# RWKV attention and mixture of experts on one core: three of four value mixes moved ahead of the weighing

## The reference

```python
shifted = pad(hidden, ((0,0),(1,0),(0,0)))[:, :-1]
key   = hidden * mix_k + shifted * (1 - mix_k)
value = hidden * mix_v + shifted * (1 - mix_v)
rec   = hidden * mix_r + shifted * (1 - mix_r)
k, v, r = key @ Wk, value @ Wv, sigmoid(rec @ Wr)
rwkv = wkv(time_decay, time_first, k, v)   # a scan over time: num and den, decayed, with a running maximum
x = layernorm(x + (r * rwkv) @ Wo)
# then, for 8 experts of width 16, the two best by a softmax router
x = layernorm(x + sum_e gate_e * (silu(x @ down_e) @ up_e))
```

## Time and profile before

| | us |
|---|---|
| median of 3 runs | 463.04 (462.94 to 463.28) |
| the profiled execution | 463.04 |
| its span | 461.3 |
| TensorE busy | 446.1 |
| VectorE busy | 405.6 |
| ScalarE busy | 355.6 |
| GpSimd busy | 315.0 |

### The profile page before, as it was taken

One profiled execution on the slowest core, in us unless ns is written; L12 is line 12 of the kernel. 1 busy time (PEld: TensorE's weight loads), 2 busy tenths in 40 slices (PEclk: granted clock), 3 DMA queues, 4 the chain that ended last, 5 costly groups with the idle time before them and its releaser, 6 DMA issues.

```text
span 461.3 us, 6679 instructions
## 1 busy us (share of the span) xinstructions
PE 446.1 (97%) x1984; PEld 339.9 (74%) x1984; DVE 405.6 (88%) x615; ACT 355.6 (77%) x801; POOL 315.0 (68%) x301
## 2 busy tenths in 40 slices
PE   8999999998999999999999999999999999999993
PEld 3444656776888878888888888888888888888761
DVE  5989998879988999999899999989898996975976
ACT  1666766785788888888788897888798887768695
POOL 2454776397758798579967797569965695754334
PEclk9999999999999999999999999999999999999997
DMA  8603220033000032100420032100420022400016
GB/s 236 222 0 118 91 91 1 1 95 112 1 1 0 2 136 92 47 0 32 153 92 0 1 137 92 48 0 23 148 93 14 1 69 93 136 1 0 0 48 227
DMA packets 20244, 30.64 MB, mean 66 GB/s; under 512 B 2032, under 2 KB 7152, under 8 KB 20208
## 3 DMA queue, kind: packets, MB, share of 16 engines
q1 hardware_dynamic: 20208, 30.21, 19.7%
HBM read 21.82 MB, written 8.39 MB: 65 GB/s over the span
## 4 chain that ended last, share of the span: by engine, by line
PE 56%; POOL 7%; DVE 7%; ACT 4%; issue 3%; POOLq 0%; ACTq 0%; DVEq 0%
PE PH L442 4%; PE PV L325 4%; PE PV L329 4%; PE PV L326 4%; PE PR L329 4%; PE PP L352 4%; PE PP L353 4%; PE PP L357 4%; PE PK L325 4%; PE PR L325 4%; PE PK L329 4%; PE PK L326 4%; PE PR L326 4%; PE PT L424 2%; ACT EX L583 2%
## 5 line engine op out<-in xcount | busy, mean ns | idle before, releaser
L583 ACT ACTIVATE PR<-PR 128x512 f32<-128x512 f32 x128 | 74.4, 582 | 24.5 <-PE PR L311 7.9
L1195 POOL TENSOR_TENSOR DQ<-DEN,EX 128x512 f32<-128x512 f32 x32 | 41.3, 1290 | 21.1 <-DVE DEN L862 21.1
L1201 POOL TENSOR_SCALAR NM<-SUM,RS 128x1 f32<-128x1 f32 x30 | 8.6, 285 | 60.1 <-ACT RS L583 60.1
L916 DVE SCALAR_TENSOR_TENSOR KT<-D,VEC,XT 128x512 f32<-128x512 f32 x57 | 47.2, 874 | 0.0
L325 PE MATMUL PK<-KH,WKH 128*128 128x512 f32 x112 | 46.2, 413 | 0.6 <-DVE NUM L879 0.6
L325 PE MATMUL PR<-RH,WRH 128*128 128x512 f32 x112 | 44.6, 399 | 1.6 <-DVE RW L903 1.6
L325 PE MATMUL PV<-VH,WVH 128*128 128x512 f32 x112 | 45.6, 407 | 0.0
L329 PE MATMUL PR<-RL,WRH 128*128 128x512 f32 x112 | 44.3, 395 | 0.7 <-POOL RL L1163 0.6
L583 ACT ACTIVATE EX<-PK 128x512 f32<-128x512 f32 x32 | 19.1, 598 | 32.8 <-DVE PK L855 32.7
L1163 POOL TENSOR_TENSOR RL<-D,RH 128x512 fp32r<-128x512 f32 x28 | 40.2, 1462 | 6.1 <-ACT RH L583 6.1
L329 PE MATMUL PV<-VL,WVH 128*128 128x512 f32 x112 | 43.9, 392 | 0.0
(11 more groups left out here) (274 smaller groups left out, 1287.8 us busy)
## 6 DMA issues: line engine op xcount, KB each, us to landing
XT<-in_xt SPq DMA_DIRECT2D x32, 256.0 KB, 3.6
XN<-in_x SPq DMA_DIRECT2D x28, 256.0 KB, 2.6
out<-XN SPq DMA_DIRECT2D x28, 256.0 KB, 2.0
X1T<-in_wo SPq DMA_DIRECT2D x1, 1024.0 KB, 5.1
XT<-in_x SPq DMA_DIRECT2D x4, 256.0 KB, 4.4
out<-XT SPq DMA_DIRECT2D x4, 256.0 KB, 2.4
X1T<-in_wk SPq DMA_DIRECT2D x2, 256.0 KB, 4.8
XN<-in_wv SPq DMA_DIRECT2D x2, 256.0 KB, 5.5
```

The costliest lines, as they stand in the source:

```text
L583: eng.activation(*a, **k).then_inc(q[s], 1)
L916: eng.scalar_tensor_tensor(out=full(b, which, c), in0=D[:, c, :], scalar=VEC[:, 2 + which, c:c + 1], in1=XT[:, c, 0:T], op0=ALU.mult, op1= ...
L1195: eng.tensor_tensor(DQ[:, :], DEN[:, 0:T], EX[:, 1, :], ALU.add).then_inc(q["e"], 1)
```

## The change

In VectorE's list, slots 4b + 2 for b = 1 to 6 (slots 6, 10, 14, 18, 22, 26), the four value mixes of batch b + 1 stood together behind weigh and the residual. Now two stand ahead of where the gate is in slots 4 to 6, which from slot 8 on is just behind lead; the third stands ahead of weigh, and the fourth stays. No instruction is added or taken away, and the waits of each are the same. The lists of TensorE, ScalarE and SyncE are the same, and so is GpSimd's but for line numbers.

```diff
@@ -1079,6 +1079,8 @@
                     gate_top(k)
                 if s == 2:
                     mixes(1, 0, 3)
+                if j == 2 and b:
+                    mixes(b + 1, 1, 0, 1)
                 if j == 3 and b:
                     mixes(b + 1, 2, 1)
                 if s != C - 1 and not 8 <= s < C * LAST:
@@ -1086,7 +1088,7 @@
                 if s == 1:
                     mixes(1, 0, 0, 1, 2)
                 if j == 2:
-                    mixes(b + 1, 1, *(() if b else (0, 1)))
+                    mixes(b + 1, 1, *((2,) if b else (0, 1)))
                 if j == 3:
                     mixes(b + 1, 2, *((2, 3) if b else (0,)))
                 if s == U - 1:
@@ -1103,7 +1105,7 @@
                 if j == 0 and b:
                     mixes(b + 1, 0, 0, 1, 2)
                 if j == 2:
-                    mixes(b + 1, 1, *(range(C) if b else (2, 3)))
+                    mixes(b + 1, 1, *((3,) if b else (2, 3)))
                     if s < U - 2 and batch(b - 2):
                         residual2(t2)
                 if j == 3:
```

## The result

| | before | after |
|---|---|---|
| median, us | 463.16 (462.94 to 463.74, 4 runs) | 467.61 (467.50 to 468.09, 4 runs) |
| ratio | | 1.0096, 95% interval 1.0079 to 1.0113 |
| span of the profiled execution | 461.3 | 465.8 |
| TensorE busy | 446.1 | 448.6 |
| VectorE busy | 405.6 | 416.1 |

The change costs 4.45 us. First the page of the changed kernel: busy time by engine, to hold against the earlier trace rows, and the chain that ended last.

A forecast was written before the change was run, and what follows sets the result against it. TensorE, 97% busy, was taken as the bound, without slack at slot 12. 2.35 us by slot 12 plus 3.3 in later batches took the 461.3 span to 466.95, so 468.7 us; range 466.5 to 470.5.

The forecast's parts named there:

- The bound and the place of the loss: TensorE bounds from slot 12 on; slack there is zero, 0.88 at slot 16 and 1.10 at slot 20.
- The alternation: A mix waits for GpSimd's subtraction in progress, then runs some 0.6 us; the next subtraction waits some 0.5 for it.
- rival (c): GpSimd keeps the port through its whole KL run, mixes enter only at its end; about 469.9 us, chance 0.05.
- Slot 6: Idle 2.21 us ahead of weigh fill with lock waits; +0.25 us at slot 8, bounds -1.0 and +1.3.
- D mixes, RH and RL still follow in the same order, and by the same alternation: After slot 6: RL ends some 0.3 us later, so TensorE's 1.42 us wait for weigh 7 shrinks only by tenths.
- By slot 12: Loss of 2.35 us: 2.1 from slot 10's late residual delaying the square and GpSimd's queue, plus 0.25 from slot 6.
- The later batches: Moves in slots 14, 18, 22, 26 cost 0.73 at slot 16, 0.85 each at slots 20, 24, 28: 3.3 us.
- (a): Only the first loss is real; later batches regain slack of 0.9 to 1.1 us; 465.4 us, chance 0.12.
- (b): Each later batch keeps slot 10's price of 2.1 us, 5.6 for the four; 471.0 us, chance 0.08.
- (d): Faster: collisions cost little, slot 10's residual fits the square's 2.1 us of room; 461.6 us, chance 0.08.

The follow-up runs named there:

- the run with slot 10 alone: Changed kernel's moves made in slot 10 only, the other five slots as in the kernel before: 464.99 us against 463.14, ratio 1.0040.
- the run with two mixes ahead: Changed kernel, but in slots 10 to 26 only two of four value mixes stand ahead of weigh: 464.37 us, ratio 1.0029 to the kernel before.
- With one mix: Changed kernel, but in slots 10 to 26 only one value mix stands ahead of weigh: 463.07 us against 463.21 for the kernel before.
- three that don't collide: Changed kernel's order, but in slots 10 to 26 the three early mixes read PR in PSUM, not XT: 462.88 us against 463.14 before.

## Why the prediction was right, point by point

**The bound and the place of the loss: right.** TensorE had no slack at slot 12 and about 1 us in the batches behind it, and the loss is where the prediction put it: at slot 12 and then at the twelfth matmul of slots 16, 20, 24 and 28. Between them nothing else delays TensorE by more than some tenths.

**The alternation: right to a tenth.** From lead to weigh in slot 10 the sum had 4.1; 4.04 was measured. The square was to come 2.0 later; against lead's end it did by 1.94 (152.95 - 147.59, before 151.60 - 148.18). KL x4 grew by 0.47 with one mix between them and by 0.91 with two, so a queued subtraction gives way at once. This refutes rival (c), that GpSimd keeps the port to the end of its run; in slot 6 the gate, behind two mixes, starts at 96.93, and the run ends at 98.17.

**Slot 6: right that nothing is won, the sign of the rest wrong.** The sum had +0.25 for the side engines, and they came out 0.3 ahead. The step that failed is "D mixes, RH and RL still follow in the same order, and by the same alternation": with GpSimd's slot 7 shifted by its late start, the first D mix met no subtraction any more (0.75 in place of 1.49), while DQ was slowed instead (1.78 in place of 1.27). The gate wasn't waiting for DQ, but the VL behind it came later, and TensorE waited for VL at value 8. TensorE's 1.42 us did not "shrink by some tenths"; the wait went and two others came, together 1.1. One of them, for WRL behind the longer KL run, has no term in the sum.

**By slot 12: 2.35 forecast, 2.05 measured** (171.45 against 169.40). VectorE was 0.28 ahead at slot 6 already, before any moved instruction (lead 7 starts at 91.64, before at 91.92), so the change itself costs 2.3 there. But the path is another one than I named. Value 12 was to stall 1.6 and stalled 0.7. RL ended at 170.55, early enough. TensorE waited for weigh 11, because the three D mixes of slot 11 collided with GpSimd three times (4.69 in place of 3.49). The sum had this part as 2.1, with D mixes that collide as before. In the run with slot 10 alone, where slot 6 is as before, they take 3.47, RL is what TensorE waits for, and the cost is 1.7: the term as I had worked it out, 2.1, was 0.4 too large. There the square comes 1.81 later (153.41 against 151.60), gate 11 1.73 (161.40 against 159.67) and RL's end 1.71 (171.05 against 169.34), where the sum had 2.0 for the square and 2.1 for the gate.

Why weigh 11 is so late in the changed kernel stays open. GpSimd's normalisation (XN<-XN,RS,ZERO, which reads one SBUF tile) and the first of the three D mixes start there within 0.04 us of each other, in every trace. This is it in the run with slot 10 alone:

```profile
163.86 1.27 POOL L1211 TENSOR_SCALAR XN<-XN,RS,ZERO 128x512 f32<-128x512 f32 x1
```

It takes 1.27 or 1.28 in slot 11 of the other eight traces, and in slots 15 and 19 of the changed kernel, and the three mixes take 3.47 to 3.50: by the durations the mix gets in first. Only in slot 11 of the changed kernel it is 0.76 and 4.69, so there the normalisation does. The moves of slots 6 and 10 together are not shown to be the reason, since the run with two mixes ahead has both and comes out like the others. What decides so near a tie wasn't tried.

So 2.05 comes near 2.35 partly by luck. Two terms were too large: slot 6 (+0.25, and it gave 0.3 back) and slot 10 (0.4). RL alone would have let the matmul start at about 170.6; the late weigh 11, which the sum didn't have, adds some 0.85 (an estimate from 170.55 and 171.45).

**The later batches: 3.3 forecast, 2.4 measured.** The mechanism is the one worked out: zero slack at each end of batch, so the side engines' time is the batch's. The size, 3.3, is 0.9 too large, in two places. Slot 16 costs 0.21 (224.73 - 171.45 = 53.28, before 53.07) and not 0.73, because RL was 0.9 ahead of TensorE at slot 12, when weigh and not RL was late. The other three cost 0.72, 0.72 and 0.71, where the sum had 0.85: in slot 14 weigh stands 3.48 behind lead's end where the sum had 3.6, and the square comes 1.38 later against lead (206.99 - 202.19, before 203.93 - 200.51), not 1.5.

Sum: 2.05 + 0.21 + 2.15 = 4.41, span 4.5, median 4.45, forecast 5.65.

**The rivals.** (a), slack takes the later batches, fell with the batches of 53.67. It would have held with two mixes, where a batch is 53.0. (b) fell with 0.7 a batch. (d), the faster one, named the right condition: it decides on whether what stands ahead of the residual takes less than 2.1 us. With one mix, or with three that don't collide, it does, and there nothing is lost; yet nothing measurable is won even then, since TensorE's waits move to other places.

None of the versions tried is measurably faster than the kernel before.

## What to carry to other kernels

Before moving an instruction into another engine's gap, look at what its neighbour does in that gap: a mix that read two SBUF tiles and GpSimd's instructions took turns here, one by one, and such a wait shows as a longer instruction, not as idle time. Compare the duration of the same instruction beside a busy neighbour and beside an idle one; the difference is the price of one collision.
An instruction that is moved costs nothing until the first one behind it comes later than its reader can take it. Find that reader's room (here 2.1 us, between the residual's end and the square), and where the bound engine has no slack, the whole excess reaches the end.

## What the runs showed of the hardware

- A mix of 512 columns takes 0.66 us from its start to the next instruction's where it meets nothing (152.84 to 153.50 in slot 10 of the changed kernel, recorded as 0.74). Beside a run of GpSimd subtractions it is recorded with up to 1.8 (1.76 for one, 3.44 for two), and each subtraction that has to wait for one takes some 0.45 to 0.5 more (KL x4 5.04, 5.51 and 5.94 with none, one and two mixes between them).
- With its second input in PSUM the same mix takes 0.66 beside the same run (three in 1.98 from the first's start to weigh), and the run isn't slowed (5.05). The gate, which also has one input in PSUM, takes its 0.69 beside the KL run too (96.93 in slot 6).
- A GpSimd instruction with one SBUF tile as its input collides as well: the normalisation takes 0.76 where it gets in first, and 1.27 or 1.28 beside the same mix otherwise.
- Such a wait shifts the collisions behind it, on both engines: the first D mix of slot 7 met a subtraction in the kernel before (1.49) and none in the changed one (0.75), with no change in the order there.
